# A Mamba-2 mixer with a routed low-rank FFN: the order of the products inside a slot, the banks they use, and the place of the y chain

## What is computed

```python
proj = hidden_states @ in_proj_w.T              # 512 -> gate 8192, hBC 8192 + 2048, dt 128
gate, hBC, dt = jnp.split(proj, [INTER, INTER + CONV_DIM], axis=-1)
hBC = silu(causal depthwise conv of 4 taps + bias)      # hs 8192, B 8 x 128, C 8 x 128
dt = softplus(dt + dt_bias);  X = hs * dt;  A_dt = -exp(A_log) * dt     # per head, chunks of 128 tokens
Y_diag = (C B^T * exp(segsum(A_dt))) X          # within a chunk
states = B^T (decay * X), carried from chunk to chunk
Y_off  = C @ previous state * exp(cumsum A_dt)
y = Y_diag + Y_off + D * hs
xg = y * silu(gate)
xr = xg * rsqrt(mean(xg * xg over 1024 channels) + EPS)      # 8 norm groups
out = (xr * norm_weight) @ out_proj_w.T
```

## Time and profile before

| | us |
|---|---|
| median of 3 runs | 1695.9 (1695.87 to 1696.78) |
| the profiled execution | 1696.02 |
| its span, first to last instruction | 1694.3 |
| TensorE matmul busy | 1644.4 (97%) |
| DVE busy | 1352.8 (80%) |
| ACT busy | 1191.2 (70%) |
| POOL busy | 1089.1 (64%) |
| mean granted TensorE clock | 0.994 of full |

### The profile page before, as it was taken

How to read it: one execution, slowest core, us unless ns; L and a number is a source line. 1 busy time by engine, 2 the same in 40 slices (tenths; PEclk the granted TensorE clock), 3 DMA queues, 4 the chain that set the end, 5 groups by cost and what they waited for, 6 DMA issues and landing times.

```text
span 1694.3 us, 28881 instructions
## 1 busy us (share of the span) xinstructions
PE 1644.4 (97%) x9694; PEld 1355.9 (80%) x9694; DVE 1352.8 (80%) x2388; ACT 1191.2 (70%) x2442; POOL 1089.1 (64%) x1384
## 2 busy tenths in 40 slices
PE   6999999999999999999899999999999999999996
PEld 5778888888888888887787788888888888888885
DVE  5987788878787888878889878888788878787875
ACT  2577777777777777777635777777777777777773
POOL 5346676676676677676663466776766676676673
PEclk9999999999999999999999999999999999999998
DMA  4243444343444344343123433443443443443331
GB/s 150 65 143 123 140 136 129 130 144 122 129 144 127 125 144 131 120 144 131 58 86 100 156 128 124 144 131 120 144 132 122 142 133 120 142 133 126 136 119 36
DMA packets 82146, 212.03 MB, mean 125 GB/s; under 512 B 11024, under 2 KB 27408, under 8 KB 81744
## 3 DMA queue, kind: packets, MB, share of 16 engines
q1 hardware_dynamic: 82000, 210.20, 38.1%
HBM read 207.01 MB, written 3.15 MB: 124 GB/s over the span
## 4 chain that ended last, share of the span: by engine, by line
PE 69%; DVE 19%; ACT 6%; issue 5%; POOL 0%; DMA 0%; SPq 0%; DVEq 0%; ACTq 0%; POOLq 0%
PE bg L509 18%; PE bh L509 16%; PE bo L676 15%; DVE cv L701 6%; PE by L641 6%; PE bt L635 4%; PE bt L657 4%; DVE mt L928 2%; PE bt L687 2%; DVE acc L719 2%; ACT raw_o L396 1%; ACT mt L390 1%; DVE xt L873 1%; ACT cv L282 1%; DVE by L918 1%
## 5 line engine op out<-in xcount | busy, mean ns | idle before, releaser
L440 POOL TENSOR_TENSOR wl<-raw,wh 128x256 fp32r<-128x256 f32 x584 | 530.6, 939 | 101.5 <-ACT wh L278 101.5
L491 POOL TENSOR_TENSOR wol<-raw_o,woh 128x256 fp32r<-128x256 f32 x256 | 184.3, 741 | 468.6 <-ACT woh L407 468.6
L701 DVE SCALAR_TENSOR_TENSOR cv<-bh,par_sb,cv 128x511 f32<-128x511 f32 (+2 forms) x408 | 304.6, 747 | 140.2 <-ACT cv L282 135.1
L291 ACT ACTIVATE mt<-cs_row,cs_tok 128x128 f32<-128x128 f32 x1024 | 324.4, 389 | 0.0
L676 PE MATMUL bo<-woh,xh 128*128 128x512 f32 x512 | 213.7, 417 | 0.0
L676 PE MATMUL bo<-woh,xl 128*128 128x512 f32 x512 | 202.6, 396 | 0.0
L676 PE MATMUL bo<-wol,xh 128*128 128x512 f32 x512 | 200.9, 392 | 0.0
L908 DVE SCALAR_TENSOR_TENSOR sg<-tg,bg 128x512 f32<-128x512 f32 x128 | 88.1, 688 | 140.6 <-ACT tg L401 140.6
L287 ACT ACTIVATE bh<-cv 128x512 f32<-128x512 f32 x136 | 81.9, 602 | 159.2 <-DVE cv L701 159.2
L479 POOL TENSOR_TENSOR xl<-xg,xh 128x256 fp32r<-128x256 f32 x256 | 181.7, 730 | 4.9 <-ACT xh L364 4.9
L364 ACT ACTIVATE xh<-xg 128x512 fp32r<-128x512 f32 x128 | 81.0, 633 | 142.8 <-DVE xg L922 142.8
(11 more groups left out here) (159 smaller groups left out, 3328.3 us busy)
## 6 DMA issues: line engine op xcount, KB each, us to landing
raw<-in_w_step SPq DMA_DIRECT2D x128, 512.0 KB, 3.7
cs_row<-cs_rows SPq DMA_DIRECT2D x128, 512.0 KB, 4.5
raw_o<-in_w_out SPq DMA_DIRECT2D x128, 256.0 KB, 2.7
ec_row<-ec_rows SPq DMA_DIRECT2D x256, 96.0 KB, 3.7
raw<-in_w_bc SPq DMA_DIRECT2D x16, 512.0 KB, 3.6
acc<-in_x SPq DMA_DIRECT2D x2, 1024.0 KB, 5.7
mt<-in_w_ffn SPq DMA_DIRECT2D x2, 1024.0 KB, 6.7
out_dram<-acc SPq DMA_DIRECT2D x2, 1024.0 KB, 4.6
```

The costliest lines, as they stand in the source:

```text
L291: e = act.activation(mt[:, m % 2, h, chunk(j)], cs_row[:, m % 2, h, chunk(j)], ACT.Relu, bias=cs_tok[:, b, j, 2 * m + h:2 * m + h + 1], sc ...
L440: e = pool.tensor_tensor(wl[:, n % 2, part], raw[:, n % 2, part], wh[:, n % 2, part].bitcast(F32), ALU.subtract)
L491: e = pool.tensor_tensor(wol[:, 1 - u, part], raw_o[:, 1 - u, part], woh[:, 1 - u, part].bitcast(F32), ALU.subtract)
L701: dve.scalar_tensor_tensor(out=cv[:, u, k:], in0=src[:, 0:L - k], scalar=par_sb[:, un % UNITS, TAPS - 1 - k:TAPS - k], in1=cv[:, u, k:], o ...
```

## The change

Inside a slot, TensorE's order becomes: conv(m), gate(m), output(m-2), at a group's end the sums of squares, states(m-1), y(m-1), transposes(m), off(m-1). conv and the transposes of block m now go to bank bh for even m and bt for odd m (`mine`), and states(m-1) to the other of the two (`other`), so that xd, xt, the state steps and the copy of S read `other`. off goes to bg, behind sg. Its three chunks wait one by one for the copy of S and for the state steps. The sums of squares go to bg as well.

The y chain (yo, by, xg) of block m-2 is now at the head of DVE's slot m; mt(m-1) comes behind xd, xt and add_group; the three taps follow one another; sg comes before h2, and the two state steps and y1 are last. Statistics and norms of the next batch come a slot later (61 to 63). ACT does last tap early, then gate's tanh, conv's tanh, raw_o, woh, the copy of S, and then the second rises and exp. POOL splits the weights of slot m+1, ahead of wol, instead of those of m+2 behind it. SP's own code is unchanged. In slot 64 the four `turn_tokens` come first, `project_dt` stands between y and off, and `project_ag` moves to the head of slot 65.

The diff, cut (moved lines are shown where they arrive):

```diff
-        bank_b, bank_c, bank_t = (bh, bt), (bg, by), (bh, bg)
+        bank_b, bank_c, bank_t, bank_s = (bh, bt), (bg, by), (bh, bg), (bh, bt)
...
@@ ACT, slot m @@
+                    mine, other = bank_s[u], bank_s[1 - u]
+                    if m == STEPS and b + 1 < NB:
+                        token_hi(b + 1, 0)
+                        token_hi(b + 1, 1)
                     if has(m - 2):
                         act.wait_ge(v_xg, did(n - 2))
                         act.wait_ge(t_out, did(n - 4))
                         act.activation(xh[:, u, :], xg[:, u, :], ACT.Copy).then_inc(a_xh, 1)
+                    if m == STEPS and b + 1 < NB:
+                        token_hi(b + 1, 2)
+                        token_hi(b + 1, 3)
+                    if has(m):
+                        act.wait_ge(t_hs, did(n))
+                        last_tap(un, u, mine)
+                        if m == 0:
+                            take_b(b, GROUPS - 2)
+                    if has(m - 2):
...
                         rises(b, m, 0)
-                        act.wait_ge(t_hs, did(n))
-                        last_tap(un, u, bh)
+                        act.wait_ge(t_g, did(n))
+                        act.wait_ge(v_sg, did(n - 1))
+                        act.activation(tg[:, :], bg[:, :], ACT.Tanh, scale=0.5).then_inc(a_tg, 1)
+                        tanh_conv(un, u, mine)
...
                         act.activation(woh[:, 1 - u, :], raw_o[:, 1 - u, :], ACT.Copy).then_inc(a_woh, 1)
+                        act.wait_ge(t_st, did(n - 1))
+                        act.wait_ge(t_off, did(n - 2))
+                        act.activation(S[:, 0, :], other[:, 0:P], ACT.Copy).then_inc(a_s1, 1)
+                    if has(m):
+                        rises(b, m, 1)
+                        act.wait_ge(a_rl, did(n, 2))
+                        act.activation(mt[:, u], mt[:, u], ACT.Exp, scale=-1.0).then_inc(a_ex, 1)
...
 @@ POOL, slot m @@
+                    if m >= -1 and (has(m + 1) or (m < STEPS + 1 and b + 1 < NB)):
+                        split_lo(step(b, m + 1))
                     if has(m - 1):
                         pool.wait_ge(a_woh, did(n - 1))
...
-                    if m + 2 < STEPS or (m < STEPS and b + 1 < NB):
-                        split_lo(step(b, m + 2))
...
 @@ TensorE, slot m @@
+                    ends = has(m - 2) and (m - 2) % PER_GROUP == PER_GROUP - 1
...
                     if has(m):
                         pe.wait_ge(p_wl, did(step(b, m)))
-                        pe.wait_ge(v_h2, did(un - 1 if m else un - 4))
-                        project(bh, b, step(b, m) % 2, 0).then_inc(t_hs, 1)
+                        if m < 2:
+                            pe.wait_ge(v_h2, did(un - 4 + m))
+                        project(mine, b, step(b, m) % 2, 0).then_inc(t_hs, 1)
...
+                        else:
+                            pe.wait_ge(v_sg, did(n - 1))
+                        if has(m - 2):
+                            pe.wait_ge(v_off, did(n - 2))
                         project(bg, b, step(b, m) % 2, 1).then_inc(t_g, 1)
...
+                    elif b + 1 < NB:
+                        pe.wait_ge(v_off, did(n - 2))
+                        if m == STEPS:
+                            for j in range(NJ):
+                                turn_tokens(b + 1, j)
+                        else:
+                            project_ag(b + 1)
+                    if ends and m > STEPS:
+                        sum_squares(bt)
                     if has(m - 2):
                         first = (m - 2) % PER_GROUP == 0
                         pe.wait_ge(p_xl, did(n - 2))
...
                         mm.then_inc(t_out, 1)
+                    if ends and m < STEPS:
+                        pe.wait_ge(v_sg, did(n))
+                        sum_squares(bg)
+                    if has(m - 1):
+                        g = (m - 1) % GROUPS
+                        pe.wait_ge(v_xd, did(n - 1))
+                        pe.wait_ge(v_x, did(n - 1))
...
+                        for c in range(NS):
+                            mm = pe.matmul(other[:, chunk(c)], btok[:, g, c, :], xd[:, c, :], start=True, stop=True)
+                        mm.then_inc(t_st, 1)
+                        pe.wait_ge(v_m, did(n - 1))
+                        pe.wait_ge(v_xg, did(n - 2))
...
+                        mm.then_inc(t_d, 1)
                     if m == STEPS and b + 1 < NB:
                         project_dt(b + 1)
                     if has(m):
                         pe.wait_ge(v_h2, did(un))
...
+                        for j in range(NJ):
+                            mm = pe.transpose(mine[:, chunk(j)], h2[:, u, chunk(j)], ident[:, :])
+                        mm.then_inc(t_t, 1)
+                    if has(m - 1):
+                        pe.wait_ge(v_sg, did(min(n, b * STEPS + STEPS - 1)))
+                        pe.wait_ge(v_off, did(n - 2))
...
+                        for c in range(NS):
+                            if c == 0:
+                                pe.wait_ge(a_s1, did(n - 1))
+                            else:
+                                pe.wait_ge(v_s, did(n - 1, 4, 2 * c))
+                            mm = pe.matmul(bg[:, chunk(c)], S[:, c, :], ct[:, g, chunk(c + 1)], start=True, stop=True)
+                        mm.then_inc(t_off, 1)
...
 @@ DVE, slot m @@
+                    if has(m - 2):
+                        dve.wait_ge(t_off, did(n - 2))
+                        dve.wait_ge(ld_ec[u], 2 * landed(n - 2))
+                        dve.tensor_tensor(yo[:, :], bg[:, 0:NS * P], ec_row[:, u, :], ALU.mult).then_inc(v_off, 1)
...
+                        dve.tensor_tensor(by[:, P:], by[:, P:], yo[:, :], ALU.add).then_inc(v_add, 1)
...
+                        dve.tensor_tensor(xg[:, u, :], by[:, :], sg[:, u, :], ALU.mult).then_inc(v_xg, 1)
+                    if m == STEPS and b + 1 < NB:
+                        token_lo(b + 1, 0)
+                        token_lo(b + 1, 1)
...
                     if ended is not None:
                         add_group(b, ended)
+                    if has(m - 1):
+                        dve.wait_ge(a_ex, did(n - 1))
...
+                        dve.tensor_tensor(mt[:, 1 - u], mt[:, 1 - u],
+                                          gt[:, (m - 1) % GROUPS, :].unsqueeze(1).broadcast_to([P, 2, L]),
+                                          ALU.mult).then_inc(v_m, 1)
...
                     if has(m):
-                        tap(un, u, bh, 1)
+                        for k in range(1, TAPS):
+                            tap(un, u, mine, k)
...
+                        dve.wait_ge(a_tg, did(n))
+                        dve.scalar_tensor_tensor(out=sg[:, u, :], in0=tg[:, :], scalar=1.0, in1=bg[:, :],
+                                                 op0=ALU.add, op1=ALU.mult).then_inc(v_sg, 1)
+                        dve.wait_ge(t_t, did(n - 2))
...
+                        silu_conv(un, u, mine, h2[:, u, :])
...
                     if has(m - 1):
...
                         dve.wait_ge(a_s1, did(n - 1))
-                        next_state(b, m - 1, 1)
-                    if has(m):
-                        tap(un, u, bh, 2)
-                        tap(un, u, bh, 3)
-                    if has(m - 1):
+                        next_state(b, m - 1, 1, other)
                         dve.wait_ge(v_s, did(n - 1, 4, 2))
-                        next_state(b, m - 1, 2)
+                        next_state(b, m - 1, 2, other)
...
-                    if b + 1 < NB and m == STEPS - 4:
+                    if b + 1 < NB and m == STEPS - 3:
                         norm_stats(b + 1)
-                    if b + 1 < NB and STEPS - 3 <= m < STEPS - 1:
+                    if b + 1 < NB and STEPS - 2 <= m < STEPS:
                         for j in range(2):
-                            norm(b + 1, 2 * (m - (STEPS - 3)) + j)
+                            norm(b + 1, 2 * (m - (STEPS - 2)) + j)
```

More of the change, by code:

```diff
@@ L616, in _, with sum_squares @@
                     n, un, u = b * STEPS + m, b * UNITS + 2 * GROUPS + m, m % 2
+                    mine, other = bank_s[u], bank_s[1 - u]
+                    ends = has(m - 2) and (m - 2) % PER_GROUP == PER_GROUP - 1
+                    def sum_squares(dst):
+                        pe.wait_ge(p_sqa, squares(b, m - 2))
+                        for j in range(NJ):
+                            mm = pe.matmul(dst[:, j:j + 1], sqa[:, chunk(j)], ones[:, 0:1],
+                                           start=True, stop=True)
+                        mm.then_inc(t_ss, 1)
@@ L650, in _ @@
                             scores(b, GROUPS - 1)
-                    if m == STEPS and b + 1 < NB:
-                        turn_tokens(b + 1, 2)
-                        turn_tokens(b + 1, 3)
-                    if has(m - 1):
-                        pe.wait_ge(v_s, did(n - 1, 4))
-                        for c in range(NS):
```

(21 more changed lines are left out.)

134 lines of the change are left out of this document (32 added, 102 removed).

## The result

The changed kernel takes **1707.1 us** (median of 4 runs, 1706.26 to 1708.85) beside 1696.1 for the kernel before on the same chip (1695.87 to 1696.78). The ratio is 1.0063, with an interval of 1.0051 to 1.0075: slower by 11 us, where I forecast 7.

The account below looks back on a forecast made before the run. TensorE was taken to set the pace. The sum was 1696.0 + 0.1 (loop of batch 1) - 3.8 (loop of batch 0) + 5.1 (joint) + 3.9 + 1.7 (end) = 1703 us, range 1690 to 1716.

Parts of the forecast that it names:

- The ordinary slot: Slot without a group's end before it: TensorE's groups sum to 11.20 us, 0.09 below the old slot, all waits gone.
- The 0.3 us of cover for the last state step: Ordinary slot: state steps end at 10.5 us, the last off product wants them at about 10.9; the thinnest cover.
- rival (d): Ordinary slots wait too: S's start 0.5 later, 98 slots lose 0.2 each, 20 us, 1723 us; chance 0.13.
- The slot behind a group's end: add_group ahead of mt and taps delays h2 and S's copy: slot about 12.9 us, losing 1.7, 7 per batch.
- rival (a): The slot with add_group does not lose, as DVE has more room: faster, 1679 us, half of it 1691; chance 0.17.
- mt to 7.1: In the slot after a group's end, DVE runs accs from 3.1 to 5.8 us, then finishes mt at 7.1.
- The loops: From conv of slot 2 to conv of slot 63: batch 1 701.3 against 701.2 us, batch 0 702.9 against 706.7.
- 1.6 in all: Batch 0's loop: loss from the next batch's statistics ahead of yo, through gate, output and the late chain; 5.5 us now.
- The joint: Between the batches: the softplus chain starts 31.9 us after conv(63), the first FFN product 47.8, not 42.7; loss 5.1.
- A lower clock in the joint would then lie under this wait: Joint between batches: a clock drop would be hidden by the first FFN product's wait for add_group.
- The 36.7: Joint between batches: TensorE is through its work 36.7 us after conv(63) instead of 34.
- The end: After the last conv: output(62) idles TensorE 4.4 us, last sums begin at 26.8, now 22.7; loss 3.9 plus 1.7 clock.

Follow-up runs that it names:

- Experiment 8: experiment 3's kernel, with GpSimd forming wl only after VectorE's mt in the 14 slots behind a group's end: ratio 0.9978, 1693.7 us.
- experiment 3: Changed kernel, with ScalarE copying the first state before scaling and rounding the output weights in the 14 slots behind a group's end: ratio 1.0019.
- experiment 4: Changed kernel, with the output product behind y and off in the last-but-one slot of each batch: ratio 1.0007.
- experiment 6: Changed kernel, with one more fp32 transpose between the fp32r conv and gate products in each of 124 slots: ratio 1.0143, 1720.7 us.

## Why the prediction was right, and which terms were off

**Sign and range** held (1703 forecast, 1707.1 measured, 1690 to 1716).

**The ordinary slot** was forecast from groups of the old trace at 11.20 and is 11.17. The 0.3 us of cover for the last state step held: off takes 0.59 there, so rival (d) did not come. Output's cover for xl was smaller than laid out, since xl ends 5.3 us after conv's start and not at 4.9; hence the 2.72 to 2.78. The 0.98 that the forecast took as the most a GpSimd piece can take was a mean: in an ordinary slot before, three weight pieces took 0.73 to 0.74 and the one that met mt 1.72. The second piece of xl takes 1.73 now.

**The slot behind a group's end** is the point that made it slower, and it lost 2.0, not 1.7; rival (a) fell. The step that was mis-sized is "mt to 7.1": mt was taken as 1.3 us and takes 1.75. I had seen it at 1.38, 0.17 of which was a wait for a GpSimd piece, and taken the duration with it into a place where it meets GpSimd at another moment and waits 0.53. Experiment 8 shows the cause. In the slot itself the late copy of S costs the 0.8 that the forecast had; what was wrong is that this could be had back in full. With the copy early DVE's own length sets the slot, and the next slot pays 0.28 (experiment 3).

**The loops**: +0.1 forecast for batch 1, +0.9 measured; 7 x 0.3 from the term above, less 0.03 in each of 54 other slots, give 0.5 of that difference. Batch 0: -3.8 forecast, -2.5 measured. Of the difference of 1.3 the same 0.8 is in it; the rest is "1.6 in all" for the statistics. Batch 0 is 2.1 longer than batch 1, as slot 62 takes 13.67, 2.5 more than an ordinary one.

**The joint** was forecast at +5.1 and is +5.2, in part by luck. The chain starts 30.2 after conv(63), not 31.9, and so the FFN product 46.4, not 47.8; the half clock in the FFN product behind the wait of 2.62 brings the rest (3.4 us at half cost 1.7). "A lower clock in the joint would then lie under this wait" was wrong: it fell behind the wait, not under it. The 36.7 at which TensorE was to be through does not follow from the terms beside it (34 - 2.5 + 4.6 = 36.1); no other term uses it.

**The end** was forecast at +5.6 and is +6.7. Output(62) was idle for 5.1 us, not 4.4, as xl takes 2.39 beside DVE's mt and not two free pieces; and the half clock costs 2.5 on output(62), not 1.7. The last sums come 29.9 after conv(63), not 26.8. (The step from 22.7 to 26.8 is 4.1, of which the forecast counted 3.9.)

On chained vector instructions the Trainium skill (VectorE: DVE Perf Modes, The DRAIN you can't avoid) has semaphores between them free. Three taps take 2.31 in every slot of the changed kernel too, 0.77 each from start to start, against 0.66 for add_group's instructions, so the trace still disagrees. But the taps differ from add_group's instructions in two things, the wait on a semaphore and the need of the result before. No run separates them.

On the clock, a granted clock of 0.51 and 0.50 followed TensorE's idle 5.1 and 5.5 us of the end, and 0.76 its 2.6 us of the joint; with waits of 3.1 and 0.8 in experiment 4 less was lost. The Trainium skill (TensorE: Matmul & The Clock Gate, Why this matters for your kernels) asks for no gaps between bursts, and these rows agree. A gap is not all there is to it: in both kernels the clock also fell to half in the joint at the products of 68 columns (860.9 before, 858.8 after), and TensorE's longest wait in the 10 us ahead was 0.76 and 0.65 us.

**What stays open**: why the changed kernel lost 2.6 us in its first prologue, to the clock as it seems, and whether it does in each execution. And GpSimd and VectorE were kept apart only in the 14 slots; in the ordinary slots, at the statistics and at the end it was not tried. What the clock did is read from traces; no run changed it alone.

## What to carry to other kernels

When TensorE sets the pace, look at the slot that has one instruction more than the others on the second engine: an order that is better in all other slots lost to the one before through 14. Write that slot's chain out by itself, and move the rare work, or what stands beside it, before the order is judged. And when a moved instruction gets its duration from the old trace, ask which engine worked beside it there, which does now, and which of the two begins first.

## What was not expected of the hardware

**VectorE's mt and GpSimd's pieces take turns.** mt is the only vector instruction of a slot that reads two arrays from SBUF. GpSimd's pieces are tensor_tensors on SBUF too. Whichever comes second waits, and its recorded time holds the wait. First an ordinary slot of the changed kernel, then the slot of experiment 3 in which mt comes first:

```profile
415.42 0.74 POOL L479 TENSOR_TENSOR xl<-xg,xh 128x256 fp32r<-128x256 f32 x1 [2.90 <-ACT xh L368]
415.66 1.59 DVE L908 TENSOR_TENSOR mt<-mt,gt 128x1024 f32<-128x1024 f32 x1
416.12 1.73 POOL L479 TENSOR_TENSOR xl<-xg,xh 128x256 fp32r<-128x256 f32 x1
```

```profile
411.06 1.22 DVE L914 TENSOR_TENSOR mt<-mt,gt 128x1024 f32<-128x1024 f32 x1
411.20 1.67 POOL L485 TENSOR_TENSOR xl<-xg,xh 128x256 fp32r<-128x256 f32 x1 [2.30 <-ACT xh L368]
```

In the changed kernel 126 of the 128 mt begin while a piece is in work, and each ends 1.08 us after that piece. A piece that begins during an mt ends 0.58 to 0.61 us after it, in all twelve profiled kernels. Alone mt takes 1.22 us and a piece 0.72 to 0.76, and an mt that begins first keeps its 1.22 beside GpSimd. So it is a question of who is first and by how much: behind a group's end mt began 0.67 us before the end of a piece and took 1.75. (The 1.27 for which the expectation of experiment 8 has GpSimd idle began 0.19 before the end of a piece.) The mean of mt is 1.36 in the kernel before and 1.59 in the changed one. GpSimd's groups in the loop of batch 0, first before, then after (count | busy us, mean ns):

```profile
L440 POOL TENSOR_TENSOR wl<-raw,wh 128x256 fp32r<-128x256 f32 x246 | 232.0, 973 | 0.0
L479 POOL TENSOR_TENSOR xl<-xg,xh 128x256 fp32r<-128x256 f32 x122 | 86.4, 728 | 0.0
```

```profile
L440 POOL TENSOR_TENSOR wl<-raw,wh 128x256 fp32r<-128x256 f32 x244 | 178.7, 762 | 0.0
L479 POOL TENSOR_TENSOR xl<-xg,xh 128x256 fp32r<-128x256 f32 x122 | 140.7, 1173 | 191.3 <-ACT xh L368 191.3
```

One piece a slot is held by mt: a weight piece before, the second piece of xl after. The taps, which read PSUM and SBUF, keep 2.31 to 2.32 with and without GpSimd beside them, and the weight pieces beside them keep their 0.74. So the changed order moves the loss from a piece with cover to one without.

**A fp32 transpose between two fp32r products is nearly free in time** (0.03 us from start to start), and the product behind it pays 0.13 (experiment 6). Read both before a change of format is priced.
